# Scores for the maxima eleven units ahead of the softmax instead of ten, in an attention and expert kernel

## The reference

```
xn  = layernorm(x)
out = x + attention(xn) + moe(xn)

attention: 16 heads of width 8, rope on q and k, causal, at most 64 tokens back
  scores = q k^T / sqrt(8), masked;  attn = softmax(scores);  y = attn v;  y @ Wproj^T + bproj
moe: 8 experts, each token takes the best two of its gates, weighted by their softmax
  h = gelu(xn @ w1[e] + b1[e]);  out += w_e * (h @ w2[e] + b2[e])
```

## Time and profile before

| | us |
|---|---|
| median of 3 runs | 764.87 |
| lowest and highest of them | 759.67, 767.23 |
| span of the profiled execution, first to last instruction | 707.8 |
| mean granted TensorE clock in it | 0.961 |

### The profile page before, as it was taken

How to read it: one execution, slowest core, us unless ns; L and a number is a source line. 1 busy time by engine, 2 the same in 40 slices (tenths; PEclk the granted TensorE clock), 3 DMA queues, 4 the chain that set the end, 5 groups by cost and what they waited for, 6 DMA issues and landing times.

```text
span 707.8 us, 26391 instructions
## 1 busy us (share of the span) xinstructions
PE 639.5 (90%) x10175; PEld 515.1 (73%) x10175; DVE 480.9 (68%) x1366; ACT 357.6 (51%) x681; POOL 371.5 (52%) x461
## 2 busy tenths in 40 slices
PE   7677999887989899899989899999999999999885
PEld 3455677655666567666667799999998999996653
DVE  6877797899888688879877344444444444446874
ACT  1354767544556466566556344444444444446552
POOL 1673352246667577777650444545454545453453
PEclk7698999999999999999999999999999999999997
DMA  8578768846878778777687867777777676784988
GB/s 257 180 199 233 207 188 222 221 141 188 252 215 238 218 208 227 217 210 210 193 224 225 249 198 247 237 239 238 242 239 235 225 253 226 251 236 110 312 255 261
DMA packets 156236, 157.92 MB, mean 223 GB/s; under 512 B 20224, under 2 KB 131096, under 8 KB 156112
## 3 DMA queue, kind: packets, MB, share of 16 engines
q1 hardware_dynamic: 141576, 135.29, 66.1%
q0 software_dynamic: 8416, 17.51, 7.2%
q10 hardware_dynamic: 6120, 3.43, 1.8%
HBM read 102.19 MB, written 58.61 MB: 227 GB/s over the span
## 4 chain that ended last, share of the span: by engine, by line
PE 63%; DVE 18%; DMA 8%; issue 6%; SPq 3%; POOL 1%; ACT 0%; ACTq 0%; DVEq 0%
PE ps L762 16%; PE ps L749 15%; DVE mx L1004 7%; PE ps L697 6%; PE ps L632 4%; PE ps L639 3%; PE ps L605 3%; PE ps L681 2%; PE ps L616 2%; DMA QK<-stack 2%; PE ps L725 2%; PE ps L735 2%; PE ps L674 2%; DMA xn<-slots_x 1%; PE ps L567 1%
## 5 line engine op out<-in xcount | busy, mean ns | idle before, releaser
L1298 POOL DMA_INDIRECT chosen_y<-xn,to x135 | 129.2, 957 | 136.4 <-DVE xn L1072 111.3
L1004 DVE TENSOR_REDUCE mx<-ps 128x8 f32<-128x1024 f32 x128 | 156.3, 1221 | 52.4 <-PE ps L639 51.9
L1205 ACT ACTIVATE hb<-ps,xn 128x256 f32<-128x256 f32 x284 | 113.2, 461 | 142.3 <-PE ps L749 142.2
L1183 ACT ACTIVATE PT<-ps 128x1024 f32<-128x1024 f32 x128 | 131.1, 1024 | 88.2 <-PE ps L681 88.1
L1292 POOL DMA_INDIRECT slots_x<-xn,pos x128 | 126.2, 986 | 57.8 <-issue 31.7
L762 PEld LDWEIGHTS ps<-xn,hb 128*128 128x128 f32 x1080 | 131.2, 192 | 3.9 <-ACT hb L1205 0.6
L762 PE MATMUL ps<-xn,hb 128*128 128x128 f32 x1080 | 132.1, 275 | 0.4 <-DVE xn L1066 0.4
L749 PE MATMUL ps<-xn 128*128 128x256 f32 (+1 forms) x568 | 130.1, 372 | 0.0
L749 PEld LDWEIGHTS ps<-xn 128*128 128x128 f32 x568 | 100.2, 192 | 10.3
L697 PE MATMUL ps<-PT,V 128*32 128x64 f32 (+1 forms) x3072 | 86.5, 246 | 1.7 <-ACT Os L1190 1.0
L1066 DVE TENSOR_TENSOR xn<-ps,xn 128x256 f32<-128x256 f32 x71 | 29.1, 410 | 83.3 <-PE ps L762 83.0
(11 more groups left out here) (151 smaller groups left out, 891.9 us busy)
## 6 DMA issues: line engine op xcount, KB each, us to landing
xn<-experts SPq DMA_DIRECT2D x71, 578.0 KB, 3.9
QK<-stack SPq DMA_DIRECT2D x128, 192.0 KB
stack<-sp SPq DMA_DIRECT2D x64, 192.0 KB
xn<-slots_x SPq DMA_DIRECT2D x64, 132.0 KB, 3.4
stack<-sp SPq DMA_DIRECT2D x64, 128.0 KB
xn<-chosen_y SPq DMA_DIRECT2D x32, 256.0 KB, 4.7
stack<-sp SPq DMA_DIRECT2D x64, 64.0 KB
Vc<-values SPq DMA_DIRECT2D x32, 128.0 KB
```

The lines of the kernel that those rows point to most:

```text
L1004: e.tensor_reduce(mo[:, :, :, c, t], ps[:, 0:2, :].rearrange("p g (h k) -> p g h k", k=P), AX.X, ALU.max, negate=True).then_inc(v_mx, 1)
L1183: e.activation(PT[:, u % 2, :], ps[:, stb(u):stb(u) + 2, :].rearrange("p c k -> p (c k)"), ACT.Exp, scale=SCALE).then_inc(a_exp, 1)
L1205: e.activation(hb[:, s, c, 0:m], ps[:, 2 * s + c // 2, (c % 2) * SL:(c % 2) * SL + m], ACT.Gelu, bias=b1b[:, i % NW, c:c + 1]).then_inc(a_ ...
L1298: e.indirect_dma_start(out=Ys, out_offset=bass.IndirectOffsetOnAxis(ap=to[:, i % 4, j:j + 1], axis=0), in_=yb[:, i % 4, j, :], in_offset=N ...
```

## The change

AHEAD becomes 11. Every `scores` unit stands one step sooner against everything else in the list: unit 4b, the first that reads a block's freshly loaded operands, moves from step 4b-10 to step 4b-11. `load` and `write` keep their steps, so there are two steps between a load and its first reader instead of three. The split of a block's maxima moves with the last of its units, from step 4b-7 (q % 4 of 1) to step 4b-8 (q % 4 of 0). What follows the split (`turn_m`, `mput`, `mget`) keeps its step. One group of three warming matmuls is dropped (the list has them while q is below -AHEAD), 116 instead of 115 units are scored ahead of the expert work, and TWO is 117 instead of 118. The scatters keep their step.

```diff
-AHEAD = 10
+AHEAD = 11
...
-    late = ((("turn_qk", 20), ("lo", 16), ("write", 16)), (("turn_o", -5), ("msplit", 7), ("write", 15)),
+    late = ((("turn_qk", 20), ("msplit", 8), ("lo", 16), ("write", 16)), (("turn_o", -5), ("write", 15)),
             (("qk", 22), ("turn_y", -6)), (("lo", 17), ("vload", 5), ("load", 13), ("proj", -7), ("turn_m", 5)))
```

## The result

| | median us | runs | |
|---|---|---|---|
| before | 765.0 | 20 | 757.96 to 772.22 |
| after | 769.59 | 20 | 763.41 to 782.97 |

The ratio is 1.0068 with a 95% interval of 1.004 to 1.0095: the change costs 3 to 7 us, where 16 us were forecast. It lies just inside the 1% that the prediction took as the limit of what can be told from no change. The ratio leaves out the disturbed, slower runs of each kernel, which is why it differs from that of the medians (1.0060).

The account below looks back on a forecast made before the run. PE bounds the kernel, its idle time mostly waits for the QK load; 12.8 + 3.3 + 1 + 0.5 - 1.6 = 16.0 us added to 764.87 gives 781 us. Range of 8 in 10: 768 to 793 us.

Parts of the forecast that it names:

- What bounds the kernel, and where the wait stands: Stage 208 to 376 us: 9.0 of PE's 12.7 idle us stand at a block's first scores, awaiting the QK load.
- The slot's loop: Same stage: first scores, scoresT freeing the slot, load, next first scores; takes 11.45 to 11.8 us a block.
- The write's loop: Same stage: write to reader lacks 2.65 to 3.4 us, shared by two blocks; 11.8 to 12.2 us a block.
- The clock: Rival, chance 0.13: longer waits at L632 also drop PE's clock in seven blocks, 8 us more, about 790 us.
- the one in the sum that put the profiled span against the median: Whole kernel: span 707.8 us plus 16.0 is 723.8; the median's 57.1 us above it stay untouched, giving 781 us.
- A block of PE's own work so takes about 10.5 us: Attention stage: PE's time for a block without waits, read from scores starting at 318.98 and 329.51 us.
- The stage's 12.8 us: Fifteen attention blocks, 208 to 376 us: 0.85 us added to each, 12.8 us in all, bounds 3.8 and 18.
- The start and blocks 11 and 12: Early load waits move up a step: 1 us at blocks 1 and 2, 3.3 us where SP clears slots.
- After the experts: Block 30's late load: its wait grows 2.36 us, partly paid back at the end; net 0.5 us, bounds -2 and 2.5.
- The split, -1.6 us: Four DVE instructions leave the path of the output's norm, awaited at L717; gain 1.6 us, bounds 0 and -5.
- The waits are absorbed: Rival, chance 0.13: PE's pace does not set the block, thinner traffic speeds landings to 5.9 us; 770 us.
- The load lands in time: Rival, chance 0.03: the load lands within 5.37 us, no new wait at scores, only the split's gain stays; 763 us.

Follow-up runs that it names:

- e5_fill: Kernel after (lead 11) with eight idle matmuls ahead of the load's wait at first scores of blocks 11 to 28; 735.41 us, ratio 1.0345.
- e10_before: Kernel before, unchanged (lead 10), profiled again in a group of the 763 us kind; median 762.2 us, profiled execution 763.5 us.
- e1_a11_m7: Kernel after with only the lead changed (AHEAD 11), the maxima's split left in step 4b-7; 745.31 us, 1.0453 against the kernel before.

## Why the prediction was right or wrong

*What bounds the kernel, and where the wait stands: right, for the execution read.* In the 713 us kind PE waits 15 times at L632 in the stage, 27.4 us in all, with L710 behind the wait, and the reader starts 0.09 us behind the load's landing each time.

*The slot's loop: right, and right in size at full clock.* It was put at 11.45 to 11.8 us a block; with the writes out of the way it measured 11.50. The write's loop was put at 11.8 to 12.2. Both kernels with lead 11 are at 11.8 without their slow stretches, and in e5_fill six of fifteen loads start as the writes land, so the writes have a part; that they set the pace by themselves is not shown. The forecast of 0.85 us a block stood for 12.06 us. (Its upper bound of 18 us is a slip: fifteen times 1.0 us is 15.)

*The clock: a rival that came true, in the 713 us kind.* It was given 8 us and took 0.6 to 1.1 us a block, 8 to 17 us in the stage. With it, and with 10.7 us behind step 101 where the sum had 0.5, that kind's cost is 33 us and not 16. So the forecast would have been too low in the kind that it was read from, too.

*The step that failed is the one in the sum that put the profiled span against the median*: "the median stands 57.1 us above that span, time which the change does not touch". The time outside a span is 1.8 us; nearly all of the 57 us are inside the span, behind step 28, and some 40 of them are in the very stage that the change touches. The term "A block of PE's own work so takes about 10.5 us" is about 13.8 us in the executions that were measured. The loop through the load takes 13.0 us there, so it is shorter and binds in six blocks only, for 4.0 us. The stage's 12.8 us (bounds 3.8 to 18) measured 3.2 to 5.1 us, steps 41 to 101.

*The other terms, in the 763 us kind.* The start and blocks 11 and 12, 1 + 3.3 us, measured 2.4 to 3.1 us up to step 41. After the experts, 0.5 us: 0.1 us by step 113, -0.7 to the end, against e10_before. A wait of 2.34 us stands there after, at 720.49, where before has 0.17 us at 714.76; the difference at the end is no larger than at step 101. The split, -1.6 us: nothing (e1_a11_m7, in the 713 us kind).

*The rivals.* "The waits are absorbed" gave 770 us, the time that was measured, and had the traffic thinner (174 GB/s in the stage after against 217). That is luck: it held that PE's pace does not set the block and that the change itself thins the traffic, where PE was slow and the traffic thin (173 GB/s) in the kernel before too. "The load lands in time" was nearly the case in the 763 us kind, though again not because loads are quick: PE comes later.

## What to carry to other kernels

What a lead between a transfer and its reader is worth is decided in the main by one comparison: the loop (buffer freed, transfer, reader, buffer freed again) against the engine's own work for that stretch. Write both numbers down before moving either end, and take both from the executions whose time is quoted; here the one was 10.5 or 13.8 us and the other 11.8 or 13.0. Where the span and the median stand far apart, here 57 us where all other profiles have 1.8 to 1.9, the profile and the times are of different executions, and an effect that depends on pace cannot be sized from it.

## What the runs showed of the hardware that was not expected

One program took about 713 us in three groups and about 763 us in three others (the result's own runs and two more), and no group's timed runs are a mixture; only the profile before, of the first kind, stands beside timed runs of the second. The chip alone does not decide it: chip 1 had a group of each kind. In the slower kind PE pauses, mostly for 0.3 to 0.5 us, inside runs of independent matmuls, 20.4 us at L639 and L697 in the stage. SP is late as well. In the stage of the kernel after, fourteen of fifteen loads are issued 1.2 to 2.0 us behind the end of a `scoresT`, where 0.08 us is the commonest in the 713 us kind; block 24, `scoresT` and load:

```profile
355.79 0.40 PE L681 MATMUL ps<-QK 51*128 51x64 bf16 x16
```

```profile
357.51 1.92 SPq L488 DMA_DIRECT2D QK<-stack  x4
```

Until 166 us, about when POOL's scatters start (the first at 159.9), there is 0.5 us of pauses at L639, and blocks take the same time in both kinds (block 5 to block 10: 62.6 us in the slower kind, 64.1 in the other). What makes a group one kind or the other, and whether the scatters are the cause of the pauses or only begin at the same time, was not tried and stays open.

A wait can cost more than its length. With waits of 1.8 us in the mean, one in each block, the granted clock was at its lower level, 0.50, often enough to bring the stage to 0.90, and a run of matmuls behind the wait took 1.08 us instead of 0.65. The eight idle matmuls in the wait brought it to 0.99. The Trainium skill, TensorE: Matmul & The Clock Gate, section "Part 1: The HAM clock gate (the 'warmup' mystery)", says that the throttled clock is the default and that activity releases it; the trace agrees.
